# Attention on one core: the softmax reciprocals spread by GpSimd broadcasts instead of VectorE's shuffle, and the value product issued in two halves

## The reference

```
x: [B=2, S=512, HID=512], NH=32 heads of D=16
q, k, v = proj(w_q), proj(w_k), proj(w_v)          # of layernorm(x)
scores  = einsum('bhqd,bhkd->bhqk', q, k) / sqrt(16)
attn    = softmax(scores, axis=-1)
out     = einsum('bhqk,bhkd->bhqd', attn, v)
x       = x + einsum('bse,oe->bso', out, w_o)
x       = x + moe(layernorm(x))                    # 8 experts, 2 per token
```

## Time and profile before

| | before |
|---|---|
| median of 3 runs (lowest to highest) | 628.91 us (628.89 to 630.19) |
| time of the profiled execution | 636.47 us |
| its span in the trace | 633.7 us |
| PE, DVE, ACT, POOL busy share of the span | 92%, 61%, 52%, 19% |
| mean granted TensorE clock | 0.949 |
| attention loop in steady state | about 129.5 to 255 us of the span |
| one group there | 11.35 us |

### The profile page before, as it was taken

One profiled execution on the slowest core, in us unless ns is written; L12 is line 12 of the kernel. 1 busy time (PEld: TensorE's weight loads), 2 busy tenths in 40 slices (PEclk: granted clock), 3 DMA queues, 4 the chain that ended last, 5 costly groups with the idle time before them and its releaser, 6 DMA issues.

```text
span 633.7 us, 10494 instructions
## 1 busy us (share of the span) xinstructions
PE 584.2 (92%) x3585; PEld 433.6 (68%) x3585; DVE 385.4 (61%) x689; ACT 329.2 (52%) x481; POOL 120.8 (19%) x137
## 2 busy tenths in 40 slices
PE   2999999999999999999944999999999999998993
PEld 2786673333333333324844999999999999998982
DVE  6715557899999999414456682828364555647140
ACT  5222115777777777661305555647374646565430
POOL 5000111001011010111004004233241507070312
PEclk9899996899999999999755999999999999999897
DMA  8180389257466420135723465655665664843213
GB/s 320 61 99 1 51 110 116 27 77 95 70 94 85 62 87 12 39 123 208 292 104 110 175 244 118 221 162 175 205 167 215 144 251 87 308 75 112 26 13 38
DMA packets 29496, 78.88 MB, mean 124 GB/s; under 512 B 8489, under 2 KB 8745, under 8 KB 24858
## 3 DMA queue, kind: packets, MB, share of 16 engines
q1 hardware_dynamic: 24474, 68.84, 40.6%
q0 software_dynamic: 4992, 9.64, 8.7%
HBM read 58.64 MB, written 9.80 MB: 108 GB/s over the span
## 4 chain that ended last, share of the span: by engine, by line
PE 47%; issue 28%; POOL 9%; DVE 8%; ACT 3%; DMA 2%; POOLq 1%; SPq 0%; ACTq 0%
PE ps_o L592 9%; PE ps L611 7%; PE ps L580 5%; DVE neg_max L1108 5%; PE ps L582 4%; PE ps L581 4%; POOL out L542 4%; PE ps_m L611 3%; PE ps L667 3%; POOL xn L524 3%; PE ps L623 2%; PE ps_o L731 2%; ACT probs_t L936 2%; POOL to_now L537 1%; DMA q_lo<-wq 1%
## 5 line engine op out<-in xcount | busy, mean ns | idle before, releaser
L936 ACT ACTIVATE probs_t<-ps 128x1024 f32<-128x1024 f32 x128 | 123.9, 1023 | 39.5 <-PE ps L623 38.1
L580 PE MATMUL ps<-xgT_hi,w_hi 128*128 128x294 f32 (+1 forms) x416 | 126.9, 305 | 5.3 <-DVE xgT_lo L1284 2.9
L582 PE MATMUL ps<-xgT_hi,w_lo 128*128 128x294 f32 (+1 forms) x416 | 125.8, 303 | 0.0
L581 PE MATMUL ps<-xgT_lo,w_hi 128*128 128x294 f32 (+1 forms) x416 | 125.1, 301 | 0.0
L1108 DVE TENSOR_REDUCE neg_max<-ps 128x1 f32<-128x512 f32 x171 | 111.6, 684 | 11.1 <-PE ps L611 9.0
L1297 DVE TENSOR_TENSOR act<-gate,ps 128x294 f32<-128x294 f32 x48 | 22.0, 461 | 104.6 <-PE ps L582 86.0
L580 PEld LDWEIGHTS ps<-xgT_hi,w_hi 128*128 128x128 f32 (+1 forms) x416 | 78.7, 189 | 5.9 <-DVE xgT_lo L1284 3.2
L581 PEld LDWEIGHTS ps<-xgT_lo,w_hi 128*128 128x128 f32 (+1 forms) x416 | 78.5, 189 | 0.0
L582 PEld LDWEIGHTS ps<-xgT_hi,w_lo 128*128 128x128 f32 (+1 forms) x416 | 78.0, 188 | 0.0
L611 PE MATMUL ps<-k_stack,q_stack 48*128 48x512 f32 x171 | 74.3, 470 | 3.1 <-issue 0.3
L592 PE MATMUL ps_o<-probs_t,v_ones 128*32 128x512 f32 x512 | 70.8, 626 | 0.3 <-ACT probs_t L936 0.3
(11 more groups left out here) (249 smaller groups left out, 959.8 us busy)
## 6 DMA issues: line engine op xcount, KB each, us to landing
w_sb<-w SPq DMA_DIRECT2D x18, 1024.0 KB
w_sb<-w SPq DMA_DIRECT2D x9, 1536.0 KB
w_sb<-w SPq DMA_DIRECT2D x9, 1152.0 KB
q_stack<-q_hi SPq DMA_DIRECT2D x32, 128.0 KB, 5.1
k_stack<-k_hi SPq DMA_DIRECT2D x32, 128.0 KB, 4.8
q_stack<-q_lo SPq DMA_DIRECT2D x16, 128.0 KB, 4.8
k_stack<-k_lo SPq DMA_DIRECT2D x16, 128.0 KB, 5.9
q_hi<-o_norm SPq DMA_DIRECT2D x16, 128.0 KB, 4.0
```

The source lines that it names most:

```text
L580: pe.matmul(o, x_hi, w_hi, start=start, stop=False)
L581: pe.matmul(o, x_hi, w_lo, start=False, stop=False)
L582: return pe.matmul(o, x_lo, w_hi, start=False, stop=stop)
L936: a.activation(probs_t[:, kc % 2, 2 * half:2 * half + 2, :], ps4[:, 2 * (n % 2):2 * (n % 2) + 2, :], ACT.Exp, scale=D ** -0.5).then_inc(s_ ...
```

## The change

Three things change. VectorE's shuffle is gone; in its place GpSimd makes four partition broadcasts for each group, of 128, 96, 64 and 32 partitions, the last head first, each waiting for the one before, and then its product. The row that each broadcast reads is row 0 of a head's 32 and no longer row 1. The value product of a quarter is issued as two times four matmuls of 256 queries, and the third maxima product of the quarter stands between the halves. The list of turns is adapted: "maxima" comes after three products instead of two.

```diff
@@ turns
+            lead = 2 if s < 0 else 3
-            turns += [(s + 2, u2) for u2 in range(2)]
+            turns += [(s + 2, u2) for u2 in range(lead)]
             turns += [(s + 1, "maxima")] * (s + 1 >= 0)
-            turns += [(s + 2, u2) for u2 in range(2, 4 * TPB)]
+            turns += [(s + 2, u2) for u2 in range(lead, 4 * TPB)]
@@ SyncE
                     if g >= 1:
-                        sp.wait_ge(s_sh, g)
-                    sp.dma_start(rec_row[1:P:2 * D, :], sum_rec[:, g % 2, :]).then_inc(s_rb, 16)
+                        sp.wait_ge(s_sh, GH * g)
+                    sp.dma_start(rec_row[0:P:2 * D, :], sum_rec[:, g % 2, :]).then_inc(s_rb, 16)
@@ GpSimd
             for g in range(NG):
-                pool.wait_ge(s_sh, g + 1)
+                pool.wait_ge(s_rb, 16 * (g + 1))
+                if g >= 1:
+                    pool.wait_ge(s_on, g)
+                for j in reversed(range(GH)):
+                    rows = 2 * D * (j + 1)
+                    pool.partition_broadcast(rec_all[0:rows, :], rec_row[rows - 2 * D:rows - 2 * D + 1, :],
+                                             channels=rows).then_inc(s_sh, 1)
+                    pool.wait_ge(s_sh, GH * (g + 1) - j)
                 if g >= 2:
                     pool.wait_ge(s_oc[g % 2], 16 * (g // 2))
                 pool.tensor_tensor(o_norm[:, g % 2, :], o_raw[:, g % 2, :], rec_all[:, :],
@@ TensorE
-            def pv(g, kc):
+            def pv(g, kc, part):
...
+                at = slice(part * S // 2, (part + 1) * S // 2)
                 for j in range(GH):
-                    last = pe.matmul(ps_o[32 * j:32 * j + 32, :],
+                    last = pe.matmul(ps_o[32 * j:32 * j + 32, at],
...
-                                     probs_t[:, kc % 2, j, :], start=(kc == 0), stop=(kc == TPB - 1),
+                                     probs_t[:, kc % 2, j, at], start=(kc == 0 and part == 0),
+                                     stop=(kc == TPB - 1), skip_group_check=True,
                                      tile_position=(0, 32 * j))
-                last.then_inc(s_pv, 1)
+                if part == 1:
+                    last.then_inc(s_pv, 1)
@@ TensorE, a quarter p of a step
                     key_max(ga, 4 * p + 1)
-                    if p < 2:
-                        pv(s - 1, p + 2)
-                    else:
-                        pv(s, p - 2)
+                    now = (s - 1, p + 2) if p < 2 else (s, p - 2)
+                    pv(*now, 0)
+                    key_max(ga, 4 * p + 2)
+                    pv(*now, 1)
                     if p == 0 and 0 <= s + 1 < NG:
                         max_t(s + 1)
-                    key_max(ga, 4 * p + 2)
                     scores(s, 2 * p)
@@ VectorE
-                    if u2 == 11 and g >= 0:
-                        v.wait_ge(s_rb, 16 * (g + 1))
-                        if g >= 1:
-                            v.wait_ge(s_on, g)
-                        v.stream_shuffle(rec_all[:, :], rec_row[:, :], [1] * 32).then_inc(s_sh, 1)
```

More of the change, by code:

```diff
@@ L582, in three @@
                 return pe.matmul(o, x_lo, w_hi, start=False, stop=stop)
-            def pv(g, kc):
+            def pv(g, kc, part):
                 if not 0 <= g < NG:
                     return
-                pe.wait_ge(s_ex, UNITS * g + 2 * (kc + 1))
-                if kc == 0 and g >= 1:
-                    pe.wait_ge(s_or, g)
+                if part == 0:
+                    pe.wait_ge(s_ex, UNITS * g + 2 * (kc + 1))
+                    if kc == 0 and g >= 1:
+                        pe.wait_ge(s_or, g)
+                at = slice(part * S // 2, (part + 1) * S // 2)
                 for j in range(GH):
-                    last = pe.matmul(ps_o[32 * j:32 * j + 32, :],
+                    last = pe.matmul(ps_o[32 * j:32 * j + 32, at],
                                      v_ones[:, (g // 8) * TPB + kc, (g % 8) * GH + j, :, :].rearrange("p d o -> p (d o)"),
-                                     probs_t[:, kc % 2, j, :], start=(kc == 0), stop=(kc == TPB - 1),
+                                     probs_t[:, kc % 2, j, at], start=(kc == 0 and part == 0),
+                                     stop=(kc == TPB - 1), skip_group_check=True,
                                      tile_position=(0, 32 * j))
-                last.then_inc(s_pv, 1)
+                if part == 1:
+                    last.then_inc(s_pv, 1)
             def max_t(g):
```

## The result

| | before | after |
|---|---|---|
| median (lowest to highest) of 4 runs each | 629.55 us (628.89 to 634.25) | 773.88 us (768.93 to 774.68) |
| profiled execution, its span | 636.47, 633.7 us | 774.67, 772.8 us |
| mean granted TensorE clock | 0.949 | 0.779 |
| pace of a group in the loop | 11.35 us | 19.3 us |

The ratio is 1.2256 with a 95% interval of 1.2176 to 1.2337: slower. The forecast of 762 us, with 700 to 845, was close in time. Its mechanism was not what set the pace in most of the loop, as the profile shows. The medians differ by 144.3 us and the profiled executions by 138.2, since that of the kernel before had a mean clock of 0.949 and took 636.47 us, where executions with 0.962 or 0.963 took 629.1 to 630.8.

What follows compares the result with a forecast made beforehand. It took a VectorE-TensorE chain of waits through three banks to bound the kernel. GpSimd's loads, broadcasts and product make 19.2 us a group: +137.0, -6 and +2 give +133 on 628.9, 762 us, range 700 to 845.

Steps and rivals of the forecast that it cites:

- What bounds the kernel: Attention loop: a chain of reduction, maxima and value products through three banks takes 2.69 us a quarter; VectorE and TensorE nearly full.
- The shuffle goes: VectorE in the attention loop: one instruction less per group, about 0.64 us in 12 steps, at most 7.7 us gained.
- The halves on TensorE: Value product: a second entry (0.21 us) and fixed cost (0.14) make 2.80 us a quarter, giving back the removed shuffle's gain.
- The broadcasts: GpSimd, each group: four broadcasts in sequence at 0.95 us each, 3.8 us in all, bounds 2.1 and 6.1.
- The loads: GpSimd, each group: two code reloads of 7.0 us each, ahead of the broadcasts and of the product; GpSimd's group 19.2 us.
- A: Rival for GpSimd's code switch: almost free, GpSimd's 9.2 us group hidden, VectorE sets the pace; 614 us, chance 0.04.
- B: Rival for the loop: code switch free, TensorE's 2.80 us quarters take the gain; 630 us, chance 0.03.
- D: Rival for GpSimd's load: only 4.0 us, so its group takes 13.2 us; 669 us, chance 0.07.
- All of the loop goes at GpSimd's pace, and the two edits above fall into the slack: Attention loop: GpSimd's 19.2 us a group, against 11.35, sets the pace; removed shuffle and split value product don't matter.
- the rows of maxima come later, TensorE waits for them: Start of each group's scores: SyncE ends its step later, delaying the maxima rows and TensorE, with ScalarE and VectorE; no separate size.
- Rival C: TensorE's clock in the loop: half speed granted because it idles, 11.2 us a group doubles to 22.4; 813 us, chance 0.05.
- The sum behind the loop: Last product ends 137.0 us later; behind it remaining projections save 6 us, lower clock adds 2: +133 in all.

Runs made afterwards that it cites:

- The last experiment: Kernel before with each group's shuffle split into two instructions of 256 columns, after the 12th and 16th reductions: 626.71 us, ratio 0.9943.
- late halves: Kernel before with the value product whole up to step 3, then in halves with a maxima product between from step 4: 633.80 us, ratio 1.0044.
- the run with DMAs: Kernel before with the shuffle of groups 0 to 11 replaced by four DMAs on GpSimd's queue: 681.49 us, ratio 1.077.
- the broadcasts alone: Changed kernel with the value product whole as before; GpSimd's four broadcasts and two loads a group stay: 746.38 us, ratio 1.184.
- the halves alone: Kernel before with the value product in halves and a maxima product between, shuffle kept, no broadcasts: 741.84 us, ratio 1.175.
- Back-to-back halves: Kernel before with the value product in two halves of 256 queries, one right behind the other, maxima product after both: 633.48 us, ratio 1.0027.

## Why the number held and the mechanism did not

**What bounds the kernel.** Right: a ring of three banks with the value product inside, 2.70 us a quarter, and almost no room on either engine. The last experiment drew its gain from just this reading.

**The shuffle goes.** It was worth at most 7.7 us by the prediction. Nothing of it can be seen in the changed kernel, where VectorE is busy 55% of the time from 200 to 250 us.

**The halves on TensorE.** The term was 0.35 us a quarter on top of 2.45; at the full clock it measured 2.70 in the late halves, 0.25. Of its two parts the fixed cost was right (2 x 0.57 against 0.99 is 0.15), and the entry as well (0.43); the remaining 0.1 lies in the base, and no row shows where. Whether "the split gives back what the removed shuffle gains" stays open, since no run has the halves at the full clock and no shuffle. Late halves with the shuffle are 0.4% slower. By the measured quarter TensorE would need 4 x 2.70 + 0.21 = 11.0 us without it, which as an estimate leaves 0.35 us a group of the gain. The rule of the Trainium skill, "TensorEngine Tiling (Array Packing)", section "Key Properties", that changing the tiling mode drains TensorE, fits the trace: 0.43 us at each entry where 0.21 is streaming.

**The broadcasts.** 0.95 us each was forecast; four start 0.89 us apart and record 0.80. 3.5 us instead of 3.8.

**The loads.** 7.0 us each was forecast; 5.7 to 6.2 ahead of the broadcasts and 6.7 to 7.7 ahead of the product were measured, so GpSimd's group is 17.8 to 18.0 instead of 19.2. That rules out rivals A, B and D, which asked for a switch that is free or takes 4.0 us. The path from one product to the next reciprocals was sized right, 4.0 us against 4.25 in the run with DMAs. That the configuration instruction of the earlier trace rows asked for what was already there is not shown, but it said nothing of a switch. Nor does a trace show where the code comes from: the changed kernel has 29501 DMA packets and the kernel before 29496. The range was worked out from loads of 5.3 and 9.5 us, although the text names 0.02 and 11.6 as bounds. The Trainium skill, "GPSIMD Engine Reference", section "2.1 Instruction dispatch", gives about 6 us for the first call after a load, shown by no instruction; the trace agrees for the switch ahead of the broadcasts (5.94) and shows about one microsecond more for the way back.

**The step that failed** is "All of the loop goes at GpSimd's pace, and the two edits above fall into the slack". It holds for the broadcasts alone (17.98 us a group) and not for the changed kernel, where TensorE at 1.2 GHz takes 19.3 us and GpSimd waits. The halves don't fall into slack: they alone cost 111 us. The step "the rows of maxima come later, TensorE waits for them" failed too, since it is the two buffers of `o_raw` that hold TensorE back. That 19.2 was forecast and 19.3 measured is chance, two errors with opposite signs: loads and broadcasts sized 1.4 us too high, and a lower clock, worth 1.5 us beyond GpSimd's own 17.8, left out of the sum.

**Rival C** had the right bound, TensorE at half the clock, at a chance of 0.05. Its cause was another: it took TensorE's idle time for the reason, and the halves hold the clock down where TensorE is never idle. It was also mis-sized, since it doubled all of 11.2 us. At the low clock the measured quarter is 4.75, presumably since the steps that don't stream don't double. Its counter-argument, "at that pace TensorE would be busy again", did not hold as a reason for the higher clock: TensorE is busy 50.00 of 50.00 us, and the clock is 0.50.

**The sum behind the loop.** Forecast 128.2 for the first reciprocals, measured 140.24, because the clock was low before them already: +12. Fifteen distances between products are 284.9 us, 18.99 on average, 3 less than forecast, since the last groups go at GpSimd's pace. The end of the last product moved by 436.8 - 291.45 = 145.4 us where 137.0 was forecast. Behind it, these 8 records are what is left of the projection, as forecast, but at 0.82 us each and not 0.43 (chain of waits):

```profile
436.85 2.56 DMA q_hi<-o_norm
...
439.54 6.56 PE ps L679 x8
```

The tail is 336.0 us against 342.3, -6.3, where -4 was forecast. 145.4 - 6.3 = 139.1, the difference of the spans. The medians differ by 5 us more, 144.3: the profiled execution of the kernel before was nearly 7 us above its median and that of the changed kernel 0.8, so a difference made in the traces came out too small for the medians.

## What to carry to other kernels

Ask of every wait or break that a change gives to TensorE not only what it costs at the present clock, but whether the granted clock comes back afterwards: here the same order of matmuls ran ten groups at either clock, depending on the clock at which it began. Price an engine in its ring, not by its busy time: GpSimd was 11% busy and had only 5.8 us a group to give, because its result, the reciprocals of the next group and the next rows of maxima all go through SyncE in one order. Look in the built program for instructions that nobody wrote; two kinds of GpSimd code that alternate cost more than all the work in them.

## What had not been expected of the hardware

In the run with the halves alone the granted clock stayed at 0.50 from 105 to 350 us while TensorE was recorded as busy without a gap, and the same matmuls in late halves ran at 1.00 with TensorE recorded busy 49.82 of 50.00 us. Back-to-back halves of the same size let the clock rise near 110 us. Recorded busy time thus doesn't tell which clock a stream will be granted; what does was not found. A switch of GpSimd's code cost 5.7 to 6.2 us one way and 6.7 to 7.7 us the other, and no instruction of that length shows it. After GpSimd had issued its four DMAs of one row to 32 rows, its product waited 7.6 to 8.4 us for them, and meanwhile SyncE's own DMA instructions, 0.6 us else, took up to 4.49 us.
